# Pooled inputs made one block ahead on chip, first steps and units moved into the opening, scores by row quarters

## The chip, the cores and the metric

The kernel runs on one core of a Trainium2 chip. The metric is the device time of an execution in microseconds; lower is better. The engines are TensorE (PE, with its weight loads as PEld), VectorE (DVE), ScalarE (ACT), GpSimd (POOL) and SyncE (SP, which only issues DMAs here). Each works off its own queue of instructions in order and waits for others through semaphores.

## The reference, cut to what matters

The input x is 128 sequences of 32 tokens of 128 features. Four stages follow each other:

```
# 1 pooled: hidden = x; scores = tanh(x @ W1 + b1) @ v          per sequence
mask  = prefix / postfix / all-but-self, by the sequence's prompt type
pooled = softmax(where(mask, scores, -1e30)) @ x / cnt
# 2 attention of the pooled input, 16 heads of 8 and a rope part shared by the heads
c_kv = pooled @ W_kv_down;  k, v = c_kv @ W_k_up, c_kv @ W_v_up;  q = pooled @ W_q
scores = (q k + rope(pooled @ W_q_rope) rope(c_kv @ W_k_rope)) / sqrt(40), causal
x = x + (softmax(scores) @ v) @ W_o
# 3 per sequence one of 64 matrices:  c2 = x @ W[cat] + b[cat]
# 4 mixture of 64 experts on c2, and a shared one
s = sigmoid(c2 @ gate_w.T);  sc = s + gate_bias;  groups of 8: best 4 of 8 groups by top-2 sum
cw = top 8 of what is left, s normalised, times 2.5
x = x + sum_e cw[:, e] * ((silu(c2 @ Wg_e) * (c2 @ Wu_e)) @ Wd_e) + shared(c2)
```

## The kernel before

The tokens go in 8 blocks of 512 (16 sequences, 4 tiles of 128 tokens), features on the partitions. For each block the mixture is 33 **units** (`UNITS`): 32 pairs of experts and the shared expert. A unit p has a gate product, a down product (of unit p - 3, `NH = 3`) and an up product, each three full matmuls of 512 columns, since every float32 operand is split into a high and a low part (`three`). Gate goes to PSUM bank G0 or G1, up to U0 or U1, down is summed in Y. ScalarE takes silu of the gate in its bank (L520); VectorE multiplies by the routing weight (`act_w`, L938), which comes as `cwb`, a row of `cw_scratch` in DRAM spread over the partitions by a DMA, four slots (`NCW`) deep, then by the up product (`hid`, L950); ScalarE rounds `hid` to its high part (L532), GpSimd subtracts for the low part (`hid_lo`, L631).

The attention, conditioning and routing of block b + 1 run beside the units of block b, as 33 **steps** written out by hand. In unit p each engine does step p + 5 (`AHEAD = 5`) of the next block, behind its own work for the unit; units 28 to 32 do steps 0 to 4 of the block after it. `steps_in` gives this order to every engine, SP included. The steps: 0 rotation of the rope parts; 1 to 4 keys masked by head (`k_blk`, VectorE) and queries masked by group (`q_grp`, ScalarE); 5 value product and rope scores; 6 and 8 the scores of two tiles each (TensorE), 6 to 9 their mask, maximum and subtraction; 10 the exponentials; 12 to 16 turned probabilities and products with values, 13 to 16 `att`; 17 transposes; 18 output product and x2; 19 the product with the category's matrix (`wcat`, loaded in steps 13 to 16); 20 transposes and c2; 21 gate scores; 22 to 29 routing on VectorE; 31, 32 the weights `cw` turned and stored to DRAM.

The same steps for block 0 run alone in the **opening**, ahead of the units, with the pooling of all eight blocks between them: `pool_hidden`, `pool_scores`, `pool_weights` in three groups (block 0; 1 to 3; 4 to 7), then for each block `spread` (four 32x32 transposes on VectorE), `pool_out` (four products on TensorE) and `pooled_out` (a copy on ScalarE). For blocks 1 to 7 `pooled_out` stores to `pooled_scratch` in DRAM, and SP loads `h_feat` from it at step 21. Expert weights come in 24 parts of 256 KB and a small one; `split(i)` rounds part i on ScalarE and subtracts on GpSimd, 17 before the units (`BEFORE_UNITS`), the others one per unit from unit 11. `warm(n)` are products that nobody reads.

SP's queue is in order too: in unit p it does the loads of step p + 5 first, then waits for `weighted` and issues `cwb` of unit p:

```
for step, blk in steps_in(p, following, last):
    attention_loads(step, blk)
if p < NPAIR:
    sp.wait_ge(S["weighted"], b * NPAIR + (NPAIR + p - NCW + 1))
...
    sp.dma_start(cwb[:, p % NCW, :], src).then_inc(cwb_in[p % NCW], 16)
```

## Time and profile before

| | |
|---|---|
| median of 3 runs | 749.6 us (747.75 to 752.17) |
| the profiled execution, its own time | 748.22 us |
| span of its trace | 746.4 us |
| mean granted TensorE clock over the span | 0.995 |
| busy share PE / DVE / ACT / POOL | 97 / 74 / 61 / 57% |

Times in the trace are microseconds from the start of the span, durations of one instruction are nanoseconds where it says so. The granted clock is a share of full speed: 1.00 is 2.4 GHz, 0.50 is 1.2 GHz. A float32 matmul of this program appears as two MATMUL instructions; matmuls overlap, so the distance between starts is what one costs, and ends are modelled. The profiled execution is the source of all rows; its time lies 1.4 us under the median.

### The profile page before, as it was taken

The page shows a single profiled execution, that of the slowest core. Times are in us where ns is not written, and L with a number is a line of the kernel's source. Part 1 is how long each engine was busy: PE and PEld are TensorE (multiplying, and loading weights), DVE is VectorE, ACT ScalarE, POOL GpSimd, SP SyncE. Part 2 cuts the span into 40 slices and gives each one's busy share as a digit, 9 for nine tenths or more (in the row PEclk, how much of TensorE's full clock was granted, in tenths as well). Part 3 has the DMA queues.
Part 4 walks back from the last instruction along what each step waited for, and adds up shares of the span by engine and source line. Part 5 has one row for each costly group of instructions (what it writes and reads, how often), then busy time and mean ns, then how long its engine had stood idle before and what let it go on. Part 6 is the DMA issues. An engine that isn't in the chain of part 4 may idle for free.

```text
span 746.4 us, 15904 instructions
## 1 busy us (share of the span) xinstructions
PE 721.3 (97%) x5680; PEld 560.0 (75%) x5680; DVE 549.0 (74%) x1150; ACT 453.5 (61%) x873; POOL 425.1 (57%) x349
## 2 busy tenths in 40 slices
PE   8877999999999999999999999999999999999997
PEld 6765776677777777777787777777777777887885
DVE  5796668886698756976778766987668766886664
ACT  3755865477556675567555774566754675555553
POOL 2528667566456545655555654666446564566665
PEclk9999999999999999999999999999999999999999
DMA  7495443435534453444564344443634345345441
GB/s 264 141 356 135 123 121 99 127 94 156 120 107 118 123 144 109 129 103 127 125 117 134 98 150 113 120 113 120 141 113 135 103 125 128 102 125 141 128 134 46
DMA packets 69055, 97.21 MB, mean 130 GB/s; under 512 B 8016, under 2 KB 26896, under 8 KB 68976
## 3 DMA queue, kind: packets, MB, share of 16 engines
q1 hardware_dynamic: 64512, 91.21, 44.1%
q10 hardware_dynamic: 4464, 4.98, 1.9%
q8 instruction: 45, 0.74, 0.4%
q14 instruction: 34, 0.28, 0.1%
HBM read 90.73 MB, written 4.98 MB: 128 GB/s over the span
## 4 chain that ended last, share of the span: by engine, by line
PE 73%; DVE 11%; ACT 10%; issue 3%; POOL 2%; POOLq 0%; DVEq 0%; ACTq 0%
PE U L967 20%; PE Y L967 20%; PE G L967 19%; PE A L967 12%; DVE act_w L938 3%; POOL hid_lo L631 2%; ACT s_t L395 2%; ACT hid_hi L532 2%; DVE hid L950 2%; ACT L520 1%; ACT L395 1%; DVE k_blk L678 1%; ACT G L520 1%; PE A L1031 1%; DVE spread_p L861 1%
## 5 line engine op out<-in xcount | busy, mean ns | idle before, releaser
L631 POOL TENSOR_TENSOR hid_lo<-hid,hid_hi 128x512 fp32r<-128x512 f32 (+1 forms) x264 | 342.1, 1296 | 275.1 <-ACT hid_hi L532 274.0
L938 DVE TENSOR_TENSOR act_w<-G,cwb 128x512 f32<-128x512 f32 x248 | 170.4, 687 | 100.3 <-ACT G L520 99.3
L520 ACT ACTIVATE G<-G 128x512 f32<-128x512 f32 x248 | 144.4, 582 | 140.6 <-PE G L967 137.7
L532 ACT CAST hid_hi<-hid 128x512 fp32r<-128x512 f32 (+1 forms) x264 | 162.4, 615 | 71.8 <-DVE hid L950 70.5
L950 DVE TENSOR_TENSOR hid<-act_w,U 128x512 f32<-128x512 f32 (+1 forms) x256 | 175.8, 687 | 24.1 <-PE Y L967 1.5
L967 PE MATMUL Y<-hid_hi,wd_hi 128*128 128x512 f32 (+1 forms) x264 | 107.0, 405 | 5.4 <-POOL hid_lo L631 5.1
L967 PE MATMUL G<-c_hi,wg_hi 128*128 128x512 f32 x248 | 111.8, 451 | 0.2 <-DVE act_w L938 0.2
L967 PE MATMUL Y<-hid_hi,wd_lo 128*128 128x512 f32 (+1 forms) x264 | 103.6, 393 | 0.0
L967 PE MATMUL Y<-hid_lo,wd_hi 128*128 128x512 f32 (+1 forms) x264 | 103.4, 392 | 0.0
L967 PE MATMUL U<-c_hi,wu_hi 128*128 128x512 f32 x248 | 99.0, 399 | 1.1 <-DVE hid L950 1.1
L967 PE MATMUL G<-c_lo,wg_hi 128*128 128x512 f32 x248 | 97.5, 393 | 0.0
L967 PE MATMUL G<-c_hi,wg_lo 128*128 128x512 f32 x248 | 97.4, 393 | 0.0
L967 PE MATMUL U<-c_hi,wu_lo 128*128 128x512 f32 x248 | 97.4, 393 | 0.0
L967 PE MATMUL U<-c_lo,wu_hi 128*128 128x512 f32 x248 | 97.3, 392 | 0.0
L967 PEld LDWEIGHTS Y<-hid_hi,wd_hi 128*128 128x128 f32 (+1 forms) x264 | 49.5, 187 | 28.9 <-POOL hid_lo L631 16.7
L967 PEld LDWEIGHTS U<-c_hi,wu_hi 128*128 128x128 f32 x248 | 46.5, 188 | 17.0 <-DVE hid L950 4.4
L967 PEld LDWEIGHTS G<-c_hi,wg_hi 128*128 128x128 f32 x248 | 46.6, 188 | 16.4 <-issue 6.8
L967 PEld LDWEIGHTS Y<-hid_lo,wd_hi 128*128 128x128 f32 (+1 forms) x264 | 49.5, 188 | 11.2
L967 PEld LDWEIGHTS Y<-hid_hi,wd_lo 128*128 128x128 f32 (+1 forms) x264 | 49.6, 188 | 9.6
L967 PEld LDWEIGHTS G<-c_lo,wg_hi 128*128 128x128 f32 x248 | 46.5, 188 | 10.7
L967 PEld LDWEIGHTS U<-c_lo,wu_hi 128*128 128x128 f32 x248 | 46.5, 188 | 10.7
L967 PEld LDWEIGHTS U<-c_hi,wu_lo 128*128 128x128 f32 x248 | 46.5, 188 | 9.7
(191 smaller groups left out, 900.0 us busy)
## 6 DMA issues: line engine op xcount, KB each, us to landing
cwb<-cw_scratch SPq DMA_DIRECT2D x256, 256.0 KB, 3.7
k_blk<-in_cond_w SPq DMA_DIRECT2D x112, 64.0 KB, 2.4
wg_raw<-in_we_gate SPq DMA_DIRECT2D x8, 256.0 KB, 6.0
wu_raw<-in_we_up SPq DMA_DIRECT2D x8, 256.0 KB, 6.2
wd_raw<-in_we_down SPq DMA_DIRECT2D x8, 256.0 KB, 6.6
xf<-in_x_feat SPq DMA_DIRECT2D x8, 256.0 KB, 4.2
out_feat<-y ACTq DMA_DIRECT2D x8, 256.0 KB, 3.6
h_feat<-pooled_scratch SPq DMA_DIRECT2D x7, 256.0 KB, 2.7
```

Of the source, the lines that this page charges most:

```text
L395: nc.scalar.activation(s_t[:, t, :], s_t[:, t, :], ACT.Exp, scale=ATT_SCALE)\
L520: nc.scalar.activation(gate_bank(p)[:, :], gate_bank(p)[:, :], ACT.Silu).then_inc(S["silu_done"], 1)
L532: nc.scalar.copy(hid_hi[0:n, p % NH, :], hid[0:n, p % NH, :]).then_inc(S["hi_ready"], 1)
L631: nc.gpsimd.tensor_sub(hid_lo[0:n, p % NH, :], hid[0:n, p % NH, :], hid_hi[0:n, p % NH, :].bitcast(F32)).then_inc(S["lo_ready"], 1)
L678: nc.vector.tensor_scalar(k_blk[:, h, :], A1[:, :], C["head_of_group"][:, h:h + 1], None, ALU.mult)\
L861: last = nc.vector.transpose(pool_pt[i % 2][rows, :, s, :], pool_p[rows, bass.ts(i, TILES), :])
L938: nc.vector.tensor_mul(act_w[:, p % NH, :], gate_bank(p)[:, :], cwb[:, p % NCW, :])\
L950: nc.vector.tensor_mul(hid[0:n, p % NH, :], act_w[0:n, p % NH, :], up).then_inc(S["hid_ready"], 1)
L967: return nc.tensor.matmul(dst, lhsT, rhs, **k)
L1031: last = nc.tensor.transpose((G[1] if opening(blk) else A1)[:, bass.ts(g, P)], s_t[:, t, bass.ts(g, P)], C["ident"])
```

## The change

- Blocks 2 to 7 are pooled beside the units: block b's pooled input by `spread` in step 21, `pool_out` in step 24 and `pooled_out` in step 25 of block b - 1, straight to `h_feat`. The token rows for it are loaded by SP in step 21 into the buffer of `att`, once the transposes of step 20 have read it. `pooled_scratch` is gone.
- Block 1's pooled input is made after step 18 of block 0, and its first products, rotation, keys and queries run in steps 19 to 21 of block 0. In block 0 two of the four key masks go to ScalarE (from a second key product in G1), in block 1 all four.
- Units 0 and 1 of block 0 have their gate and up products before `cw` of block 0 is there. Their weights are spread by products with `pick` into Y and A1 (`first_weights`), not by DRAM. Step 6 of block 1 moves from unit 1 to unit 2.
- Scores: instead of four masked copies of q, one copy; each product takes 32 rows (one group of four heads) and has a tile position in rows and columns. Step 6 does groups 0 and 1 of all tiles, step 8 groups 2 and 3; in block 0 all at once into four banks. Step 8 waits for both tiles of step 6.
- 11 splits instead of 17 come before the units, the rest one per unit from 11 to 24; six weight loads are issued by ScalarE's queue. The fillers of steps 21 and 31 are gone. The loads of the categories come before those of x of blocks 1 to 7.

```diff
-        s_t = sb("s_t", [P, TILES, HEADS * SEQ])
+        s_t = sb("s_t", [P, NG, TILES * HG * SEQ])
...
-        q_grp = sb("q_grp", [P, NG, TOK])
+        q_sb = sb("q_sb", [P, TOK])
...
-        xt_in = [x_early[:, 4, :], x_early[:, 5, :], act_w[:, 2, :], hid[:, 2, :], y[:, :]] \
-            + [x_early[:, i, :] for i in range(3)]
-        pooled = [h_feat[:, :]] + [k_blk[:, i, :] for i in range(4)] + [act_w[:, 2, :], y[:, :], hid[:, 2, :]]
+        xt_in = [x_early[:, 4, :], x_early[:, 5, :]] + [att[:, :, :, :].rearrange("p t h d -> p (t h d)")] * (NBLK - 2)
...
-        pool_pt = [spread_p[:, i, :].rearrange("p (t s j) -> p t s j", t=TILES, s=SPT) for i in range(2)]
+        pool_pt = sb("pool_pt", [P, TILES, SPT, SEQ])
+        pool_p = sb("pool_p", [P, NBLK * TILES, SEQ])
...
-        h_dram = nc.dram_tensor("pooled_scratch", [P, NBLK * TOK], F32).ap()
...
-        BEFORE_UNITS = 17
-        SPLIT_UNITS = range(11, 11 + NSPLIT + 1 - BEFORE_UNITS)
+        BEFORE_UNITS = 11
...
-        WARM = {9: 4, 12: 2, 13: 2, 14: 2, 15: 2, 21: 24}
+        WARM = {9: 4, 12: 2, 13: 2, 14: 2, 15: 2}
...
+            sp.dma_start(cat_row[:, :], cats.to_broadcast([CATS, NSEQ])).then_inc(S["cats_in"], 16)
+            sp.dma_start(cat_table, cond_b).then_inc(S["cats_in"], 16)
+            sp.dma_start(gbias[:, :], gate_bias.to_broadcast([P, E])).then_inc(S["cats_in"], 16)
...
-                elif p == 21 and not (isinstance(blk, int) and blk == NBLK - 1):
...
-                    sp.wait_ge(S["wo_ps"], blk + 1)
-                    if opening(blk):
-                        sp.wait_ge(S["h_stored1"], 16)
-                    elif isinstance(blk, int) and blk == 1:
-                        for i in range(2, NBLK):
-                            sp.wait_ge(S[f"h_stored{i}"], 16)
+                elif p == 21 and 0 < blk < NBLK - 1:
+
+                    sp.wait_ge(S["c2_ps"], blk + 1)
                     sp.sem_inc(S["load_turn"], 1)
-                    sp.dma_start(h_feat[:, :], h_dram[:, bass.ds(blk * TOK + TOK, TOK)]).then_inc(S["h_in"], 16)
+                    token_load(blk + 1, "xt_in")
...
-            for i in range(1, 4):
-                token_load(i, "xt_in1")
+            token_load(1, "xt_in1")
...
+            for i in range(9, NSPLIT):
                 weight_load(i)
...
-                if p < NPAIR:
+                if p < NPAIR and (prev or p >= 2):
...
-                    if p == 0:
+                    if p == (0 if prev else 2):
...
+            def key_masks(heads, blk):
+
+                act.wait_ge(S["k_again_ps" if opening(blk) else "k_ps"], 1 if opening(blk) else blk + 1)
+                wait(act, "score_tile_ps", blk * TILES)
+                for h in heads:
+                    nc.scalar.mul(k_blk[:, h, :], (G[1] if opening(blk) else A1)[:, :], C["head_of_group"][:, h:h + 1]).then_inc(S["k_ready"], 1)
+
+            def pooled_out(i):
+
+                act.wait_ge(S["pooled_ps"], i + 1)
+                if i == 1:
+                    act.wait_ge(S["v_ps"], 1)
+                elif i >= 2:
+                    act.wait_ge(S["wo_ps"], i)
+                nc.scalar.copy(h_feat[:, :], (A0 if i == 0 else G[1] if i == 1 else A1)[:, :]).then_inc(S["pooled_ready"], 1)
...
-                    nc.scalar.mul(q_grp[:, p - 1, :], A2[:, :], C["group"][:, p - 1:p]).then_inc(S["q_ready"], 1)
+                        nc.scalar.copy(q_sb[:, :], A2[:, :]).then_inc(S["q_ready"], 1)
+                        if blk < 2:
+                            key_masks((range(2, HG), range(HG))[blk], blk)
...
+                elif p == 25 and 0 < blk < NBLK - 1:
+                    pooled_out(blk + 1)
...
-                act.dma_start(h_dram[:, bass.ts(i, TOK)], pooled[i]).then_inc(S[f"h_stored{i}"], 16)
...
+            for i in range(3, 9):
+                weight_load(i)
+            pooled_out(0)
...
                     pool_exp(1)
+                elif p == EXPS:
                     split(2)
                     split(3)
...
+                elif p == 19:
+                    split(6)
+                    pool_exp(2)
                 elif p == 20:
-                    pooled_out(2)
-                elif p == ROUND:
                     round_input(0, 0)
...
+                elif p == 21:
+                    split(7)
+            attention_step(1, 1)
+            for i in range(8, BEFORE_UNITS):
+                split(i)
...
+                    dst = act_w[:, p, :] if b == 0 and p < 2 else gate_bank(p)[:, :]
+                    nc.scalar.activation(dst, gate_bank(p)[:, :], ACT.Silu).then_inc(S["silu_done"], 1)
...
+                if p == 1 and not prev:
+                    attention_step(CWT, 0)
+                    attention_step(CWT + 1, 0)
...
+                if not prev and BEFORE_UNITS <= p <= NSPLIT:
+                    split(p)
...
+            for u in range(2):
+                for i in range(2):
+                    pair = C["ident"][:, E * i + 2 * u:E * i + 2 * u + 2].unsqueeze(1).to_broadcast([P, F, 2])
+                    last = nc.gpsimd.tensor_copy(pick[:, u, i, :].rearrange("p (f two) -> p f two", two=2), pair)
+            last.then_inc(S["pick_ready"], 1)
...
-                if 12 <= p < 17:
+                if 12 <= p < 18:
                     split(p - 10)
+            rope_add(1)
             pool.wait_ge(S["cw_ready"], 1)
-            for i in range(7, 10):
-                split(i)
...
+            for i in range(8, BEFORE_UNITS):
                 split(i)
...
+                    if h < 2 or blk >= 2:
+                        nc.vector.tensor_scalar(k_blk[:, h, :], A1[:, :], C["head_of_group"][:, h:h + 1], None, ALU.mult)\
+                            .then_inc(S["k_ready"], 1)
...
+                    dve.wait_ge(S["score_tile_ps"], TILES if opening(blk) else blk * TILES + t + 1)
...
+                        ps = first_scores[:, :, bass.ts(t, P)].rearrange("p g (h k) -> p g h k", k=SEQ)
+                        bias = rope_mask[:, t, :].unsqueeze(1).unsqueeze(1).to_broadcast([P, NG, HG, SEQ])
+                    else:
...
+                        ps = (A2, A1)[t % 2][:, :].rearrange("p (t h k) -> p t h k", h=HG, k=SEQ)
+                        bias = rope_mask[:, :, :].unsqueeze(2).to_broadcast([P, TILES, HG, SEQ])
+                    chain(nc.vector.tensor_add(s, ps, bias), blk)
+                    nc.vector.tensor_reduce(head_max[:, t, :], s_t[:, t, :].rearrange("p (n k) -> p n k", k=SEQ), AX, ALU.max)\
+                        .then_inc(S["biased_tile"], 1)
...
+                    if t == 0 and blk >= 2:
+                        dve.wait_ge(S["pooled_ps"], blk + 1)
...
+                elif p == 21 and 0 < blk < NBLK - 1:
+                    spread(blk + 1)
...
-                if p == 13:
-                    pool_scores(2)
+                if p == 9:
+                    pool_weights(1)
                 elif p == 16:
-                    pool_weights(1)
                     spread(1)
                 elif p == 18:
-                    spread(2)
-                    pool_weights(2)
+                    pool_scores(2)
...
+                    rotate(1)
+                    rest_of_input(0, 0)
+            pool_weights(2)
+            attention_step(0, 1)
...
-                    dve.wait_ge(cwb_in[p % NCW], b * (16 * NPAIR // NCW) + 16 * (p // NCW + 1))
-                    nc.vector.tensor_mul(act_w[:, p % NH, :], gate_bank(p)[:, :], cwb[:, p % NCW, :])\
+                    if b == 0 and p < 2:
+                        dve.wait_ge(S["cwb_ps"], p + 1)
+                        gate, weight = act_w[:, p, :], (Y, A1)[p]
+                    else:
+                        loaded = b * NPAIR // NCW + p // NCW + 1 - (1 if p % NCW < 2 else 0)
+                        dve.wait_ge(cwb_in[p % NCW], 16 * loaded)
+                        gate, weight = gate_bank(p)[:, :], cwb[:, p % NCW, :]
+                    nc.vector.tensor_mul(act_w[:, p % NH, :], gate, weight)\
...
+                pe.wait_ge(S["pooled_ready"], blk + 1)
...
+                if opening(blk):
+                    mm(G[1][:, :], k_w[:, :], h_feat[:, :]).then_inc(S["k_again_ps"], 1)
...
-                elif p in (6, 8):
...
-                            pe.wait_ge(S["biased_tile"], blk * TILES + t - 1)
...
-                                last = mm((A2, A1)[t % 2][32 * r:32 * r + 32, bass.ts(g, P)], q_grp[:, g, tok], k_blk[:, :, tok])
+                elif p == 6 and opening(blk):
+                    pe.wait_ge(S["rope_mask_ready"], 1)
+                    pe.wait_ge(S["k_ready"], HG)
+                    pe.wait_ge(S["tanh_done"], 2)
+                    for t in range(TILES):
+                        for r in range(SPT):
+                            tok = bass.ts(t * SPT + r, SEQ)
+                            for g in range(NG):
+                                rows = slice(32 * g, 32 * g + 32)
+                                last = mm(first_scores[32 * r:32 * r + 32, g, bass.ts(t, P)], q_sb[rows, tok],
...
+                elif p in (6, 8) and not opening(blk):
+                    pair = (p - 6, p - 5)
+                    if p == 6:
+                        pe.wait_ge(S["rope_mask_ready"], blk + 1)
+                        pe.wait_ge(S["k_ready"], blk * HG + HG)
+                        if blk == 1:
+                            pe.wait_ge(S["weighted"], NPAIR + 2)
+                    else:
+                        pe.wait_ge(S["biased_tile"], blk * NG + 2)
+                    for s in range(SPB):
+                        t, r = divmod(s, SPT)
+                        for g in pair:
+                            rows = slice(32 * g, 32 * g + 32)
+                            last = mm((A2, A1)[g % 2][32 * r:32 * r + 32, bass.ts(t, P)], q_sb[rows, bass.ts(s, SEQ)],
+                                      k_blk[rows, :, bass.ts(s, SEQ)], tile_position=(32 * g, 32 * r))
+                    last.then_inc(S["score_tile_ps"], 2)
...
-                    pe.wait_ge(S["prob_tile"], blk * TILES + t + 1)
+                    pe.wait_ge(S["prob_tile"], t + 1 if opening(blk) else blk * NG + NG)
...
+                elif p == 24 and 0 < blk < NBLK - 1:
+                    pool_out(blk + 1)
...
+                    pe.wait_ge(S["xt_in1"], 16)
+                    pe.wait_ge(S["biased_tile"], TILES)
+                else:
+                    pe.wait_ge(S["xt_in"], 16 * (i - 1))
+                    pe.wait_ge(S["c2tok_ready"], i)
+                dst = A0 if i == 0 else G[1] if i == 1 else A1
...
+            for p in range(CWT):
                 attention_step(p, 0)
-                if p == 7:
+                if p == 6:
...
+                elif p == 19:
+                    pe.wait_ge(S["pooled_ready"], 2)
+                    mm(G[0][:, :], rope_w[:, :], h_feat[:, :]).then_inc(S["rope_ps"], 1)
                 elif p == 21:
-                    pool_out(3)
-                    pool_out(4)
+                    mm(A1[:, :], k_w[:, :], h_feat[:, :]).then_inc(S["k_ps"], 1)
+                    pe.wait_ge(S["tanh_gate"], 1)
+                    mm(A2[:, :], W["q"], h_feat[:, :]).then_inc(S["q_ps"], 1)
...
+            def first_weights():
+
+                attention_step(CWT, 0)
+                pe.wait_ge(S["cwT_ready"], 1)
+                pe.wait_ge(S["k_ready"], 2 * HG)
+                pe.wait_ge(S["pick_ready"], 1)
+                for u in range(2):
+                    dst = (Y, A1)[u].rearrange("p (u two n) -> p two u n", two=2, n=P)
+                    for i in range(2):
+                        last = mm(dst[:, i], pick[:, u, i, :], cw_feat[:, :])
+                    last.then_inc(S["cwb_ps"], 1)
...
+                    if not prev:
+                        pe.wait_ge(S["rot_ready"], 2)
...
+                steps = steps_in(p, following, last)
+                if not prev and p == 1:
+                    first_weights()
+                    steps = []
+                elif not prev and p == 2:
+                    steps = steps_in(1, 1) + steps
+                for step, blk in steps:
```

## Rows read from the trace of the kernel before

**Rows 1.** The page, busy time by engine (share of the span)
```profile
PE 721.3 (97%) x5680; PEld 560.0 (75%) x5680; DVE 549.0 (74%) x1150; ACT 453.5 (61%) x873; POOL 425.1 (57%) x349
```

**Rows 2.** Busy time by stretch: start:end, length, busy (instructions), clock, DMA share, GB/s
```profile
0.00:64.34 64.34, 52.21 (x736) 43.01 (x737) 47.33 (x141) 35.40 (x78) 26.50 (x30) 0.97 0.69 229
79.66:162.85 83.19, 81.05 (x587) 60.69 (x583) 62.85 (x128) 53.16 (x101) 54.99 (x46) 1.00 0.42 117
342.57:429.33 86.76, 85.59 (x669) 66.00 (x665) 65.16 (x137) 53.93 (x103) 48.76 (x40) 1.00 0.49 122
429.33:509.29 79.96, 79.42 (x586) 61.34 (x582) 59.90 (x128) 49.62 (x91) 44.58 (x36) 1.00 0.45 123
```

**Rows 3.** Timeline of VectorE in the opening: start, us, line, operation
```profile
33.27 0.68 DVE L839 SCALAR_TENSOR_TENSOR hid<-act_w,G 128x512 f32<-128x512 f32 x1
...
41.38 0.69 DVE L708 TENSOR_TENSOR x_next<-A,xf 128x512 f32<-128x512 f32 x1
...
55.79 0.42 DVE L800 TENSOR_TENSOR cw<-rt,small 128x256 f32<-128x256 f32 x1
```

**Rows 4.** Timeline of TensorE in the opening
```profile
38.73 1.12 PE L967 MATMUL A<-h_feat,w 128*128 128x512 f32 x2 [0.68 <-ACT h_feat L403]
```

**Rows 5.** Timeline of ScalarE's queue, first store of the routing weights
```profile
58.31 1.32 ACTq L424 DMA_DIRECT2D cw_scratch<-cw_feat  x2
```

**Rows 6.** Timeline of SP's queue, block 0 and block 4
```profile
61.20 1.25 SPq L352 DMA_DIRECT2D cwb<-cw_scratch  x2
...
457.09 0.34 SPq L314 DMA_DIRECT2D h_feat<-pooled_scratch  x1
457.54 10.92 SPq L352 DMA_DIRECT2D cwb<-cw_scratch  x6
```

**Rows 7.** The line that loads `cwb` (L352), whole run
```profile
DMA to landing us min/median/max: 3.0/3.7/7.7
```

**Rows 8.** Busy time by stretch, opening (columns as in rows 2)
```profile
20.00:22.00 2.00, 0.45 (x32) 0.37 (x32) 1.97 (x4) 1.91 (x8) 1.59 (x2) 1.00 0.03 8
...
24.00:26.00 2.00, 2.00 (x44) 1.85 (x40) 1.08 (x2) 1.94 (x5) 0.00 (x0) 0.50 0.87 282
```

**Rows 9.** Timeline of TensorE in block 4
```profile
417.15 1.05 PE L967 MATMUL A<-v_w,h_feat 128*128 128x128 f32 x8
...
420.80 1.96 PE L967 MATMUL A<-k_blk,q_grp 128*32 128x128 f32 x64
...
427.44 1.95 PE L967 MATMUL A<-k_blk,q_grp 128*32 128x128 f32 x64
...
450.86 0.47 PE L967 MATMUL A<-v_blk,pt_sb 128*32 128x36 f32 x32
...
462.22 0.60 PE L1074 MATMUL A<-c,att 128*128 128x128 f32 x4
...
481.03 0.47 PE L967 MATMUL Y<-hid_hi,wd_hi 128*128 128x512 f32 x1
```

**Rows 10.** Timeline of VectorE in block 4
```profile
427.28 0.69 DVE L694 TENSOR_REDUCE head_max<-s_t 128x16 f32<-128x512 f32 x1
...
464.18 0.69 DVE L938 TENSOR_TENSOR act_w<-G,cwb 128x512 f32<-128x512 f32 x1 [0.46 <-ACT G L520]
...
467.16 0.69 DVE L938 TENSOR_TENSOR act_w<-G,cwb 128x512 f32<-128x512 f32 x1 [1.50 <-ACT G L520]
...
468.56 0.61 DVE L757 TENSOR_TENSOR rt<-biased 128x128 f32<-128x128 f32 x1
...
485.44 0.42 DVE L800 TENSOR_TENSOR cw<-rt,small 128x256 f32<-128x256 f32 x1
```

**Rows 11.** Timeline of VectorE in block 0
```profile
122.50 1.32 DVE L740 TENSOR_TENSOR rt<-rt 128x64 f32<-128x64 f32 x1
123.74 0.21 DVE L741 TENSOR_TENSOR rt<-rt 128x64 f32<-128x64 f32 x1
```

**Rows 12.** Timeline of GpSimd in block 0
```profile
122.45 1.29 POOL L597 TENSOR_TENSOR wd_lo<-wd_raw,wd_hi 128x512 fp32r<-128x512 f32 x1
```

More of the change, by code:

```diff
@@ L402, in attention_step @@
                     act.wait_ge(S["attT_ps"], blk + 1)
-                    nc.scalar.copy(att_feat[:, :], A1[:, :]).then_inc(S["attT_ready"], 1)
+                    nc.scalar.copy((y if opening(blk) else att_feat)[:, :], A1[:, :]).then_inc(S["attT_ready"], 1)
                 elif p == 19:
@@ L418, in attention_step @@
                     wait(act, "cw_stored", blk * 32)
-                    nc.scalar.copy(cw_feat[:, :], A0[:, 0:TOK // 2]).then_inc(S["cwT_ready"], 1)
+                    nc.scalar.copy(cw_feat[:, :], (Y if opening(blk) else A0)[:, 0:TOK // 2]).then_inc(S["cwT_ready"], 1)
                 elif p == CWT + 1:
@@ L481, in _ @@
             pool_hidden(1)
-            act.wait_ge(S["pooled_ps"], 1)
-            nc.scalar.copy(h_feat[:, :], A0[:, :]).then_inc(S["pooled_ready"], 1)
+            for i in range(3, 9):
+                weight_load(i)
+            pooled_out(0)
             split(0)
             split(1)
-            for p in range(UNITS):
+            for p in range(CWT):
                 attention_step(p, 0)
@@ L561, in unit @@
                     nc.scalar.copy(y[:, :], x2_next[:, :]).then_inc(S["x2_moved"], 1)
-            for p in range(AHEAD):
-                attention_step(p, 1)
-            pooled_out(5)
-            pooled_out(6)
             pipeline(unit)
@@ L618, in _ @@
                 attention_step(p, 0)
-                if 12 <= p < 17:
+                if 12 <= p < 18:
                     split(p - 10)
+            rope_add(1)
             pool.wait_ge(S["cw_ready"], 1)
-            for i in range(7, 10):
-                split(i)
-            rope_add(1)
-            for i in range(10, BEFORE_UNITS):
+            for i in range(8, BEFORE_UNITS):
                 split(i)
@@ L1030, in attention_step @@
                     for g in range(NG):
-                        last = nc.tensor.transpose((G[1] if opening(blk) else A1)[:, bass.ts(g, P)], s_t[:, t, bass.ts(g, P)], C["ident"])
+                        probs = s_t[:, t, bass.ts(g, P)] if opening(blk) else s_t[:, g, bass.ts(t, P)]
+                        last = nc.tensor.transpose((U[0] if opening(blk) else A1)[:, bass.ts(g, P)], probs, C["ident"])
                     last.then_inc(S["probT_ps"], 1)
@@ L1153, in _ @@
             pool_hidden(2)
-            for p in range(STEPS):
-                if p == CWT:
-                    warm(8)
+            for p in range(CWT):
                 attention_step(p, 0)
-                if p == 7:
+                if p == 6:
                     pool_scores(2)
@@ L1225, in unit @@
                         .then_inc(S["up_done"], 1)
-                if p == 0 and not prev:
-                    pool_out(7)
-                for step, blk in steps_in(p, following, last):
+                steps = steps_in(p, following, last)
[5 more added lines that the diff above has]
+                for step, blk in steps:
                     attention_step(step, blk)
```

191 lines of the change are left out of this document (59 added, 132 removed).

## The prediction, made before the change was run

> **What bounds the kernel now.** I read the page first: TensorE is busy 721.3 us, 97% of the span of 746.4 [rows 1]. Then the busy times by stretch [rows 2]. The cuts are the gate product of unit 4 in block 0 (79.66), that of unit 2 in block 1 (162.85), and the same two points in blocks 4 and 5 (429.33, 509.29). In that last stretch, of a block in its steady state, TensorE is busy 79.42 of 79.96 us: such a block costs the sum of its TensorE work. One whole block, unit 4 to unit 4, is 429.33 - 342.57 = 86.8 us. The opening is another matter: of the first 64.34 us TensorE is busy 52.21, fillers (`warm`) among it, and VectorE 47.33. And block 0 takes 83.19 where the steady block takes 79.96: 3.2 us more, with GpSimd busy 54.99 instead of 44.58. So the change can win or lose in three places: the opening, each block's TensorE sum, and stalls inside the blocks.
>
> **The opening.** In block 0 VectorE has pooling work between the steps of attention: `pool_scores(2)` from 33.27, three operations of 0.7, stands ahead of the adds of steps 14 to 16, and `pool_weights(1)` with `spread(1)` ahead of the add of step 18, which starts at 41.38 [rows 3] although its product ended at 38.73 + 1.12 = 39.85 [rows 4]. In the change both have left these places: 2.1 us from the first, 1.5 from the second, 3.6 for x2. `pool_weights(2)` (as many operations again) also leaves the way to c2; I take 4.1 for c2. The scores of block 0 in one lot are worth little: four VectorE adds and maxima per tile, 0.7 each, set the pace. SP's three category loads now go ahead of x of blocks 1 to 3, for which I have taken 1 us off. Routing then meets `rope_add(1)` on GpSimd, which holds one short operation up for 1.1 us (see block 0 below). The weights `cw`, now done at 55.79 + 0.42 = 56.2 [rows 3], come 3.2 us sooner, at 53.0.
>
> From `cw` to unit 4 the kernel takes 79.66 - 56.2 = 23.5 us. In the change units 0 and 1 have had their gate and up products before, the rotation, keys and queries of block 1 are done, and the weights of these two units come by four products instead of DMAs. What remains, counted from `cw`: VectorE is held by `pool_weights(2)` and a lock until +2.8, while transpose, copy and two `pick` products (an estimate: 1.7) run beside it; multiplies of two units and the rope mask, four of 0.69 less overlap, +5.3; scores +6.3; one score tile, 2 x 0.7, +7.7. Meanwhile unit 2's weights go by DRAM as now: `cw_scratch` issued at +0.9, the load 2.9 us after it (58.31 to 61.20 [rows 5, 6]), 0.5 for the issue, 3.7 to land [rows 7]: +8.0. It is then the last to come. Two multiplies, one tile, second scores: +11.8. The fillers are gone: after 2 us in which TensorE was busy 0.45, the granted clock fell to 0.50 (1.2 GHz of 2.4) [rows 8], and here TensorE has little from about 51 to 57: +0.5. Unit 4 starts at 53.0 + 12.3 = 65.3, **14.4 us earlier**.
>
> **Scores in every block.** Steps 6 and 8 are 64 matmul instructions each on four column tiles, 1.88 us from their start to the next matmul's, 29 ns apiece (the rows' 1.96 has a modelled end) [rows 9]. In the change the same 64 use 32 rows each: eight tiles. The trace has nothing on different row tiles at once. Bounds: no gain (1.88), and the pace of the smallest matmuls seen, 32 in 0.47 us, 15 ns apiece, 0.94 [rows 9]. I take 1.0, since each tile streams half as much and the issue pace allows it. By the Trainium skill, TensorEngine Tiling, Key Properties and Gotcha 1, tiles work in parallel as long as row tiles write different PSUM banks, and the pair goes to A2 and A1. By that rule it is 0.94, by the row of the scores alone 1.88; no row here shows it.
> Not all is kept. Step 8 starts at 427.44 today [rows 9] and needs only the first tile by then; in the change it waits for both, and VectorE ends the second at 427.28 + 0.69 = 427.97 [rows 10]. What is ahead of it moves up with TensorE's 0.9 us from step 6, to 427.1; TensorE, ready at 426.55, waits 0.55. Net **-1.1 us** for each of attention blocks 2 to 7, which run beside unit blocks 1 to 6.
>
> **Pooling, moved from the opening into blocks 0 to 5.** `pool_out` is four products; the nearest row is 8 instructions in 1.05 us [rows 9]. `spread`, four transposes of 0.3, fits into VectorE's idle 1.50 us before 467.16 [rows 10] if nothing else is late. `pooled_out` is one copy on ScalarE, which gives back three of four query copies; neither bounds.
> What is late is a load. At unit 16 SP waits before it issues that unit's `cwb`. Today it waits for the product of step 18: h_feat is issued at 457.09, `cwb` at 457.54 [rows 6]; it lands 3.7 us on, at 461.2, and the multiply of unit 16 is at 464.18 [rows 10]: 2.9 us to spare. In the change SP waits there for `c2_ps`, the transposes of step 20, 462.22 + 0.60 = 462.8 [rows 9]: 5.8 us later. The token load goes first, `cwb` at 463.4, landed at 467.1. The multiply slips by 2.9 us. Behind it on VectorE stand hid of unit 16, `spread` (its free slot is gone), both multiplies of unit 17 and routing, 4.1 us after it: at 471.2 instead of 468.56. From 468.56 to the last `cw` (485.44) VectorE shows no idle time [rows 10], so it can't catch up, and TensorE's margin is down to nothing at 481.03, where it takes the down product as hid_lo ends [rows 9]. TensorE loses **2.6 us** in each of blocks 0 to 5; the 1.05 us of `pool_out` fall inside that time and are not added.
>
> **Block 0.** Only 11 splits come before the units instead of 17; the rest run in units 11 to 24, not 11 to 18. A routing operation that takes 0.21 elsewhere takes 1.32 [rows 11] while GpSimd subtracts (122.45, 1.29 us [rows 12]). The six more splits fall under units 19 to 24, where I count three such short operations, 0.6 each: +1.8. By the Trainium skill, SBUF, the section on the shared port, the port pair is locked for a whole instruction; by that each of them could wait 1.29, +3.9. Block 0: 1.8 + 2.6 = **+4.4**.
>
> **Sum.** -14.4 + 4.4 + 5 x (2.6 - 1.1) - 1.1 = -3.6 us on 746.4. The profiled execution took 748.2, 1.8 over its span; the median of the runs shown is 749.6. I put the sum on the median: **746.0 us**.
>
> **Rivals.**
> - *The load is hidden after all.* Blocks 1 to 5 then change by 1.05 - 1.1, block 0 by +1.8, block 6 by -1.1: -14.0 in all, **735.6**. For it: 2.9 us to spare today. Against: the release is 5.8 us later. It needs a landing within 0.8 us of the issue; the shortest seen is 3.0 [rows 7].
> - *Slower: row tiles don't overlap.* Steps 6 and 8 stay at 1.88 and step 8 waits 0.55: +0.55 instead of -1.1 in six blocks (+9.9); the opening's 128 instructions take 3.8 instead of 1.7 (+2.1): **758**. It decides if 64 instructions take over 1.6 us. For it: no row of such overlap. Against: on four column tiles instructions of 128 columns do follow each other at 29 ns.
> - *GpSimd bounds block 0.* A split and a hid_lo are 2.6 us per unit against 2.1 of TensorE's, in eight units, and GpSimd waits for VectorE besides: another +5, **751**. For it: the 3.2 us that block 0 loses already.
>
> **Chances.** The forecast 0.47 (own range 742 to 750), the hidden load 0.22, the tiles 0.11, GpSimd 0.20. The range is 735 to 757. Under 0.5% (3.75 us) a change can't be told from none here. Faster than 745.85: all of the second case and 0.23 of the first, 0.45; within: 0.24 of the first and 0.14 of GpSimd's, 0.38; slower 0.17.
>
> **What would show it.** Right: the gate product of unit 4 near 65; 64 score instructions in about 1 us; at unit 16 SP released by the transposes and VectorE idle for 2 to 3 us before act_w, ended by a DMA; blocks 1 to 5 at 88.3 us instead of 86.8, unit 4 to unit 4; short routing operations of 1.3 us as late as unit 24 of block 0. Wrong: steady blocks under 86, no wait for `cwb`, scores still at 1.88, or a clock under 1.00 beyond the first units.

## The result, and the profile after

The changed kernel takes **754.5 us** (median of 17 runs, 751.2 to 757.5) against 748.1 for the kernel before on the same chip (17 runs): ratio 1.0076, 95% interval 1.0061 to 1.0092. It is 0.8% slower. I had forecast 746.0, slightly faster; 754.5 lies inside the range of 735 to 757, but on the other side of no change. The profiled execution has a span of 750.8 us (746.4 before). Its own time, 752.6, lies 1.8 us under its median, so the two traces show 4.4 us of the 6.4 between the medians; where the other 2.0 lie no trace here tells.

Cut at the same points as before (gate product of unit 4 in block 0, of unit 2 in block 1, of unit 0 in block 7), busy time by stretch, first the kernel before where [rows 2] has no such stretch:

```profile
162.85:671.77 508.92, 504.58 (x3861) 389.66 (x3858) 382.27 (x798) 317.26 (x602) 287.30 (x230) 1.00 0.45 122
671.77:746.40 74.63, 70.02 (x304) 56.30 (x302) 46.81 (x68) 38.28 (x70) 45.17 (x35) 0.98 0.41 112
```

and the changed kernel:

```profile
0.00:70.86 70.86, 52.64 (x837) 39.70 (x837) 47.67 (x128) 38.65 (x90) 31.57 (x37) 0.95 0.57 176
70.86:159.10 88.24, 82.79 (x595) 60.34 (x591) 65.98 (x131) 55.06 (x104) 61.55 (x51) 1.00 0.48 116
159.10:676.36 517.26, 504.99 (x3902) 383.68 (x3897) 386.60 (x818) 309.95 (x593) 287.47 (x231) 1.00 0.46 119
676.36:750.80 74.44, 69.98 (x304) 56.28 (x302) 46.81 (x68) 38.33 (x70) 45.14 (x35) 0.98 0.38 115
```

| stretch | before | after | change | forecast |
|---|---|---|---|---|
| start to unit 4 of block 0 | 79.66 | 70.86 | -8.8 | -14.4 |
| to unit 2 of block 1 | 83.19 | 88.24 | +5.05 | +4.4 |
| to unit 0 of block 7 | 508.92 | 517.26 | +8.3 | +6.4 |
| to the end | 74.63 | 74.44 | -0.2 | 0 |
| sum | 746.4 | 750.8 | **+4.4** | **-3.6** |

Of the 8.0 us between the two sums 5.6 lie in the opening. In the third stretch TensorE is busy for as long as before (505.0 and 504.6 us) while the stretch is 8.3 us longer: 7.9 of them are waiting.

**The late `cwb`.** Block 4, timeline of SP's queue, then of VectorE, against [rows 6, 10]:

```profile
464.18 0.34 SPq L270 DMA_DIRECT2D att<-in_x_tok  x1
464.63 9.79 SPq L332 DMA_DIRECT2D cwb<-cw_scratch  x7
```

```profile
468.65 0.69 DVE L936 TENSOR_TENSOR act_w<-banks,cwb 128x512 f32<-128x512 f32 x1 [3.66 <-DMA cwb<-cw_scratch]
469.45 0.69 DVE L948 TENSOR_TENSOR hid<-act_w,banks 128x512 f32<-128x512 f32 x1
470.05 1.24 DVE L866 STREAM_TRANSPOSE pool_pt<-pool_p 32x128 f32<-32x128 f32 x4
471.33 0.69 DVE L936 TENSOR_TENSOR act_w<-banks,cwb 128x512 f32<-128x512 f32 x1
472.12 0.69 DVE L948 TENSOR_TENSOR hid<-act_w,banks 128x512 f32<-128x512 f32 x1
472.73 0.28 DVE L762 TENSOR_TENSOR rt<-biased 128x128 f32<-128x128 f32 x1
```

SP issues the token load and then `cwb` of unit 16 at 464.63 instead of 457.54; VectorE stands idle for 3.66 us, ended by that DMA; `spread` and the routing queue behind it. The routing starts 4.2 us later than in [rows 10] by the clock of the trace; counted from the gate product of unit 4 (430.56 here, 429.33 before) it is 2.9 us, where I had 2.6. The list of SP's waits (in total, times, longest) has the place; before, the longest at that place was 5.5 us:

```profile
SPq L301 <- PE banks L1090: 67.8, 6, 11.4
```

**The scores**, TensorE, block 4, against the 1.88 us from start to the next matmul in [rows 9]: here 1.08 (429.48 to 430.56), after a wait of 0.52 for the second tile.

```profile
429.48 1.15 PE L965 MATMUL banks<-k_blk,q_sb 32*32 32x128 f32 x64 [0.52 <-DVE head_max L694]
430.56 0.50 PE L965 MATMUL banks<-c_hi,wg_hi 128*128 128x512 f32 x1
```

**The opening.** TensorE's products on x of blocks 1 to 3; then VectorE; then GpSimd; then TensorE around `cw`:

```profile
11.11 1.39 PE L965 MATMUL banks<-x_early,w 128*32 128x128 f32 x24 [2.91 <-DMA x_early<-in_x_feat]
```

```profile
41.48 0.69 DVE L711 TENSOR_TENSOR x_next<-banks,xf 128x512 f32<-128x512 f32 x1 [1.46 <-PE banks L965]
...
44.84 0.69 DVE L714 TENSOR_TENSOR c<-banks,cat_bias 128x512 f32<-128x512 f32 x1 [0.62 <-PE banks L1090]
...
50.15 1.34 DVE L762 TENSOR_TENSOR rt<-biased 128x128 f32<-128x128 f32 x1 [2.60 <-POOL biased L578]
...
58.18 0.43 DVE L805 TENSOR_TENSOR cw<-rt,small 128x256 f32<-128x256 f32 x1
```

```profile
48.15 1.28 POOL L586 TENSOR_TENSOR wu_lo<-wu_raw,wu_hi 128x512 fp32r<-128x512 f32 x1 [2.32 <-ACT wu_hi L438]
49.39 0.73 POOL L578 TENSOR_TENSOR biased<-score,gbias 128x256 f32<-128x256 f32 x1
50.08 1.26 POOL L567 TENSOR_TENSOR rope_sum<-pt_sb 64x512 f32<-64x512 f32 x1
```

```profile
58.75 0.41 PE L1104 MATMUL banks<-c,cw 128*128 128x128 f32 x2 [3.19 <-DVE cw L805]
59.62 3.39 PE L965 MATMUL banks<-cw_feat,pick 128*128 128x256 f32 x8 [0.46 <-ACT cw_feat L418]
```

`cw` is done at 58.6, 2.4 us later than in [rows 3] and 5.6 later than my 53.0. c2 is made from 44.84 on, and the routing starts only at 50.15: GpSimd subtracts weight tile 7 before it makes the biased scores, and then adds the rotated halves (`rope_add(1)`) while the first routing operation runs, which takes 1.34 us where the like operation behind it (L763) takes 0.28.

### The profile page after: what moved, and what is told of

The parts are those of the page before. It is cut to its first block, busy times and chain, and to the rows that moved or that the text cites. A ratio compares the mean times of both kernels' runs of the same rounds, so it can differ in the third digit from the quotient of the medians.

```text
span 750.8 us, 15764 instructions
## 1 busy us (share of the span) xinstructions
PE 710.4 (95%) x5626; PEld 540.0 (72%) x5626; DVE 547.1 (73%) x1144; ACT 442.0 (59%) x854; POOL 425.7 (57%) x352
## 4 chain that ended last, share of the span: by engine, by line
PE 63%; DVE 16%; ACT 8%; issue 4%; DMA 4%; POOL 3%; SPq 1%; POOLq 0%; DVEq 0%
PE banks L965 60%; DVE act_w L936 5%; DMA cwb<-cw_scratch 4%; DVE hid L948 3%; POOL hid_lo L623 2%; ACT s_t L392 2%; ACT hid_hi L526 2%; ACT L514 1%; ACT L392 1%; ACT banks L514 1%; PE banks L1047 1%; DVE head_max L694 1%; DVE s_t L693 1%; DVE pool_pt L866 1%; DVE rt L768 1%
## 5 line engine op out<-in xcount | busy, mean ns | idle before, releaser
L936 DVE TENSOR_TENSOR act_w<-banks,cwb 128x512 f32<-128x512 f32 x254 | 174.6, 687 | 138.7 <-ACT banks L514 112.7
L514 ACT ACTIVATE banks<-banks 128x512 f32<-128x512 f32 x254 | 147.2, 582 | 127.7 <-PE banks L965 125.7
L948 DVE TENSOR_TENSOR hid<-act_w,banks 128x512 f32<-128x512 f32 (+1 forms) x264 | 181.3, 687 | 23.7 <-PE banks L965 1.5
L965 PE MATMUL banks<-c_hi,wg_hi 128*128 128x512 f32 x264 | 120.8, 458 | 7.9 <-DVE act_w L936 7.9
L965 PE MATMUL banks<-hid_hi,wd_hi 128*128 128x512 f32 (+1 forms) x264 | 107.7, 408 | 5.4 <-POOL hid_lo L623 5.2
L965 PE MATMUL banks<-c_hi,wg_lo 128*128 128x512 f32 x264 | 103.7, 393 | 0.0
L965 PE MATMUL banks<-c_lo,wg_hi 128*128 128x512 f32 x264 | 103.7, 393 | 0.0
L965 PE MATMUL banks<-hid_hi,wd_lo 128*128 128x512 f32 (+1 forms) x264 | 103.7, 393 | 0.0
L965 PE MATMUL banks<-hid_lo,wd_hi 128*128 128x512 f32 (+1 forms) x264 | 103.5, 392 | 0.0
L965 PE MATMUL banks<-c_hi,wu_hi 128*128 128x512 f32 x256 | 102.2, 399 | 0.3 <-DVE hid L948 0.3
L965 PEld LDWEIGHTS banks<-hid_hi,wd_hi 128*128 128x128 f32 (+1 forms) x264 | 49.5, 187 | 30.9 <-POOL hid_lo L623 19.1
```

The costliest lines, as they stand in the source:

```text
L514: nc.scalar.activation(dst, gate_bank(p)[:, :], ACT.Silu).then_inc(S["silu_done"], 1)
L936: nc.vector.tensor_mul(act_w[:, p % NH, :], gate, weight)\
L948: nc.vector.tensor_mul(hid[0:n, p % NH, :], act_w[0:n, p % NH, :], up).then_inc(S["hid_ready"], 1)
L965: return nc.tensor.matmul(dst, lhsT, rhs, **k)
```

## The experiments

Ratios are to the kernel before, measured beside each experiment; "unit 4", "unit 8" are the starts of these gate products in block 0, "block 0" the time from unit 4 to unit 2 of block 1.

**1. `cwb` first.** At unit 16 of the changed kernel SP's order is turned round.

```diff
-    for step, blk in steps_in(p, following, last):
-        attention_loads(step, blk)
+    if p != 16:
+        for step, blk in steps_in(p, following, last):
+            attention_loads(step, blk)
     if p < NPAIR and (prev or p >= 2):
...
+    if p == 16:
+        for step, blk in steps_in(p, following, last):
+            attention_loads(step, blk)
```

> The changed kernel, but at unit 16 SP issues that unit's cwb load before it waits for c2_ps and loads the tokens. Theory (the late cwb costs 2.6 us in each of blocks 0 to 5, and hides 1.05 us of pool_out): the idle time of VectorE before act_w(16), 3.66 us in block 4, falls under 0.5 us, the blocks from the gate product of unit 0 to the next are 1.5 us shorter (88.3 to 86.8 in block 4), 9 us in all: 745 us, ratio to the kernel before 0.997. Rival (spread and the two products of pool_out bound these blocks whatever the load does): under 3 us shorter, 752 or more.

Measured: **740.2 us**, ratio 0.9894 [0.9866, 0.9921], 14 us under the changed kernel and 1.1% faster than the kernel before. Busy time by stretch:

```profile
73.19:157.10 83.91, 81.66 (x596) 61.00 (x591) 64.69 (x131) 55.07 (x104) 62.11 (x51) 1.00 0.52 120
157.10:664.29 507.19, 500.22 (x3901) 385.54 (x3897) 387.32 (x818) 311.79 (x592) 287.73 (x231) 1.00 0.48 122
```

VectorE's idle time before act_w(16) in block 4 is 0.46 us, ended by ScalarE. From block 1 to block 7 it gives back 10.1 us, 2.0 for each of the five blocks (I had 1.5), and in block 0 alone 4.3; 14 us in all by the medians, against the 9 expected (12 by the traces, of which this one has an opening 2.3 us longer). The rival is out. The wait for the transposes has moved to `cwb` of unit 17, which now stands behind the token load, and there it costs less:

```profile
460.60 0.69 DVE L940 TENSOR_TENSOR act_w<-banks,cwb 128x512 f32<-128x512 f32 x1 [0.48 <-DMA cwb<-cw_scratch]
```

**2. The same wait in the kernel before.** There SP loads h_feat at step 21; it now waits for the transposes of step 20 (in block 0 of the attention it stays).

```diff
-    sp.wait_ge(S["wo_ps"], blk + 1)
+    sp.wait_ge(S["wo_ps" if opening(blk) else "c2_ps"], blk + 1)
```

> The kernel before with one edit: in blocks 1 to 6 SP waits at step 21 for c2_ps, as the changed kernel does, and no longer for wo_ps, before it loads h_feat and then cwb of unit 16. Theory (the later wait alone makes cwb late and costs each of blocks 0 to 5 about what the experiment with cwb first gave back there, 2 us): VectorE idle for 2 to 3.7 us before act_w(16), the blocks 2 us longer, 12 us in all: 760, ratio 1.016. Rival (it costs only together with spread, which took VectorE's free slot): under 1 us in each block, 754 or less.

Measured: 757.7 us, ratio 1.0136 [1.0113, 1.0159]. VectorE waits for the same load:

```profile
474.45 0.69 DVE L938 TENSOR_TENSOR act_w<-G,cwb 128x512 f32<-128x512 f32 x1 [3.29 <-DMA cwb<-cw_scratch]
```

Blocks 1 to 6 take 7.5 us more, 1.5 for each of five; block 0 only 0.7 (83.86). Another 2.1 us were lost in this execution's opening, which the edit doesn't touch (below). So the wait alone does most of it, without `spread`: the theory, at 8 us in the trace and not 12 (the medians differ by 9.6). But it doesn't do the 4.3 us of block 0.

**3. Block 0: GpSimd relieved, without and with the late `cwb`.** ScalarE copies the weights in the place of GpSimd's difference for tiles 11 to 23; the true low parts of these weights are left out.

```diff
     nc.scalar.copy(hi, raw).then_inc(S["split_hi"], 1)
+    if i >= BEFORE_UNITS:
+        act.wait_ge(S["split_lo"], i)
+        nc.scalar.copy(lo, raw).then_inc(S["split_lo"], 1)
...
 def split(i):
+    if BEFORE_UNITS <= i < NSPLIT:
+        return
     pool.wait_ge(S["split_hi"], i + 1)
```

> The changed kernel with cwb of unit 16 first, and GpSimd relieved in block 0: for the weight tiles 11 to 23 a copy of the weights by ScalarE stands in the place of GpSimd's difference, so the low parts of these weights are not what they should be and the time of ScalarE grows by 0.6 us in each of 13 units. Theory (GpSimd's splits lengthen short VectorE operations of the routing from 0.2 to 1.3 us): block 0 from the gate product of unit 4 to that of unit 2 in block 1 falls from 83.9 to 81, total 737. Rival (they cost nothing that TensorE sees): 83.9 and 740.

> The changed kernel, late cwb and all, with GpSimd relieved in block 0: for the weight tiles 11 to 23 a copy by ScalarE stands in the place of GpSimd's difference, so the low parts of these weights are not what they should be. The late cwb costs block 0 4.3 us (88.2 against 83.9 from the gate product of unit 4 to that of unit 2 in block 1) where a steady block loses 2.0 and block 0 of the kernel before with the late wait lost 0.7. Theory (the splits in units 11 to 24 are what keeps VectorE and GpSimd from catching up): 84.5 to 85.5 here, 3 us or more off, total 751. Rival (late cwb and splits add up, 1.3 us for the splits as in the experiment without the late cwb): 87, total 753.

Measured with `cwb` first: 736.4 us, ratio 0.9851 [0.9826, 0.9875]; from unit 8 to unit 2 of block 1, where the opening's clock no longer plays in, 73.7 instead of 75.1 us: 1.3 off, not the 3 expected. With the late `cwb`: **748.2 us**, ratio 1.0010 [0.9990, 1.0030], 6 us under the changed kernel; block 0 as a stretch:

```profile
70.55:153.93 83.38, 81.62 (x596) 60.75 (x591) 61.22 (x131) 61.50 (x117) 45.46 (x38) 1.00 0.53 122
```

That is 4.9 us less than the 88.24 of the changed kernel, and more than the theory had. The four kernels, from unit 8 to unit 2 of block 1 in us:

| | GpSimd's splits | relieved |
|---|---|---|
| late `cwb` | 79.40 | 74.53 |
| `cwb` first | 75.06 | 73.74 |

The late load costs 0.8 without the splits (0.7 in the kernel before with the late wait) and 4.3 with them; the splits cost 1.3 without the late load and 4.9 with it; both together 5.7. They don't add up. The starts of the gate products show where: counted from unit 8, the changed kernel and the one with `cwb` first are level at unit 17 (27.4 us), 1.9 us apart at unit 20 (36.7 and 34.8), 3.3 at unit 24 (48.2 and 44.9) and 4.4 at unit 27 (57.8 and 53.4), while the two relieved kernels are 0.8 apart at unit 19 and stay so. It isn't how busy GpSimd is (61.6 us in the stretch, and 62.1 in the shorter one with `cwb` first), nor the long routing operations by themselves: between units 17 and 28 eight of them take over 0.6 us in the changed kernel, 7.9 us together, and seven, 6.3 us together, with `cwb` first; yet TensorE's waits there are 4.9 us in the first and 1.3 in the second. My reading, which no run separates further: the long operations cost TensorE something only once the late load has used up VectorE's lead.

**4. The category loads behind x of blocks 1 to 3**, where they were before (three `dma_start` lines moved to `i == 4`).

> The changed kernel with the three category loads behind x of blocks 1 to 3, as in the kernel before. Theory (they are why x lands 1.9 us later, which I priced at 1 us): TensorE's wait for x_early ends near 9.3 us instead of 11.1, h_feat is copied 1.5 to 2 us earlier, the weights cw are done near 57 instead of 58.6, and the whole is 1.5 us shorter: 753. Rival (the category loads hold up something else when they come later, or GpSimd's order before the routing takes the gain): no change at cw, 754.5.

Measured: 751.9 us, ratio 1.0034 [1.0016, 1.0053]: 2.6 us less by the medians, as the theory had it; by its profile `cw` is 1.9 us earlier and unit 4 1.1, but unit 8 no earlier at all (79.70), and the span is 750.9. These two profiles don't show what the runs do: this one lies 0.8 us over its median, that of the changed kernel 1.8 under. How far it is the loads can be read over all profiled executions: the 24 products on x of blocks 1 to 3 start at 11.1 to 12.2 us in the eight with the category loads ahead (h_feat copied at 16.1 to 18.2), and at 9.2 to 10.9 in the six with them behind (14.3 to 17.3). About 1.7 us, under a scatter of nearly the same size: in experiment 2, whose opening is that of the kernel before, h_feat came at 17.33 instead of 14.27.

**5. GpSimd's order.** rope_add(1) ahead of the biased add, split 7 behind `cw`.

```diff
+    if p == 20:
+        rope_add(1)
     attention_step(p, 0)
-    if 12 <= p < 18:
+    if 12 <= p < 17:
         split(p - 10)
-rope_add(1)
 pool.wait_ge(S["cw_ready"], 1)
-for i in range(8, BEFORE_UNITS):
+for i in range(7, BEFORE_UNITS):
     split(i)
```

> The changed kernel, but on GpSimd in the opening rope_add(1) goes ahead of the biased add, and split 7 goes behind cw, with splits 8 to 10. Theory (routing of block 0 is late by GpSimd's order): the first routing operation starts near 48.9 instead of 50.15 and takes 0.3 instead of 1.34, cw is done near 56.3 instead of 58.6, the gate product of unit 4 comes 2.3 us earlier, 68.6 instead of 70.9, total 752. Rival (the four splits behind cw, 5 us of GpSimd, hold hid_lo of unit 0 and the multiplies up): unit 4 not earlier than 70, total 754 to 755.

Measured: 753.6 us, ratio 1.0073 [1.0049, 1.0097], no change by the runs. The routing does start at 48.48 and its first operation takes 0.29 us; `cw` is done at 55.88, 2.7 us earlier, and unit 4 at 69.78, but unit 8 at 79.82. Of the 2.7 us 0.9 are c2, which this execution has at 43.91; the edit's own part is 1.8 (from c2 to `cw` 12.0 us instead of 13.8). Busy time by stretch shows where it went; the clock is the third column from the end:

```profile
54.00:56.00 2.00, 0.00 (x0) 0.01 (x1) 1.83 (x7) 1.46 (x5) 0.04 (x1) 0.83 0.00 0
56.00:58.00 2.00, 1.52 (x4) 1.05 (x5) 1.90 (x4) 0.37 (x1) 2.00 (x2) 0.50 0.00 0
...
66.00:68.00 2.00, 0.31 (x2) 0.00 (x0) 1.86 (x4) 0.97 (x3) 1.01 (x2) 1.00 0.24 62
68.00:70.00 2.00, 1.67 (x65) 1.29 (x66) 1.68 (x4) 0.72 (x3) 1.96 (x2) 0.74 0.37 122
70.00:72.00 2.00, 2.00 (x5) 1.59 (x6) 1.26 (x2) 0.54 (x1) 0.00 (x0) 0.50 0.38 117
```

Twice TensorE has nothing to do for 2 us or more, and twice the granted clock falls to 0.50 (1.2 GHz of 2.4). The second time it waits for the score tiles ahead of step 8, and the products of unit 4 then take 0.63 us instead of 0.40.

**6. Fillers.** Products of 128 columns nobody reads, ahead of the rope scores of block 1, ahead of the transposes of `cw`, and (in the second of the three) ahead of step 8.

> The changed kernel with cwb of unit 16 first, and fillers on TensorE: 22 of 128 columns ahead of the rope scores of block 1 and 26 ahead of the transposes of cw, 0.11 us each. Theory (in the experiments without them the clock fell to 0.50 for 6 to 11 us, at a different place each time, and took away what an edit of the opening had gained): the clock stays at 1.00 from 44 to 66, the eight pick products take 1.7 instead of 3.4 us, the gate product of unit 4 comes at 69 to 70.5 instead of 73.2, total 738. Rival (cw and the load of cwb(2) set unit 4 at any clock): unit 4 at cw + 12.3 as before, total 740.

> The changed kernel as it is, late cwb and all, with fillers in the three places: 10 ahead of the rope scores of block 1, 12 ahead of the transposes of cw, 6 ahead of step 8 of block 1. Theory (leaving the fillers out cost the opening two spells at half the clock): the clock at 1.00 from 44 to 80, the pick products 2.0 instead of 3.4 us, the gate product of unit 8 at 78 instead of 79.7, total 752 to 753. Rival (the opening is bound by VectorE and the load of cwb(2), and the fillers only take TensorE's time): 79.7 or later, 754.5 or more.

> The kernel before with the 24 fillers of step 21 left out, one part of the change alone. Theory (they hold the clock through the routing of block 0): the clock falls to 0.50 somewhere between 55 and 70 for 4 to 10 us, and the gate product of unit 4 comes 1.5 to 3 us later than 79.7, total 750 to 751. Rival (the forecast's half microsecond, since VectorE and the loads set this stretch): 80.2 or less, 748.6.

The first missed: 744.8 us, ratio 0.9962 [0.9945, 0.9979], 4 us worse than without fillers. A filler takes 0.22 us, not the 0.11 that I had read off a grouped row whose count is not one per product: the transposes came 4.5 us late for them, and the clock still fell at 73, ahead of step 8. With the right numbers, on the changed kernel: the clock stays at 1.00 from 44 to 82 and the pick products take 1.99 us instead of 3.39; yet 753.6 us, ratio 1.0062 [1.0043, 1.0081], within the uncertainty of the changed kernel's 1.0076. And the kernel before without its 24 fillers is as fast as with them: 748.3 us, ratio 1.0004 [0.9990, 1.0019], with a clock of 0.50 from 58 to 64 and unit 4 at 79.67. Leaving the fillers out cost nothing that these runs can tell, there or here.

**7. One row quarter after the other.** In steps 6 and 8 the loops over row quarters and sequences are exchanged; the instructions are the same 64.

```diff
-for s in range(SPB):
-    t, r = divmod(s, SPT)
-    for g in pair:
+for g in pair:
+    for s in range(SPB):
+        t, r = divmod(s, SPT)
```

> The changed kernel, but in steps 6 and 8 of blocks 1 to 7 the 32 matmuls of the first row quarter are all issued before the 32 of the second, instead of in turn; work and results are the same. Theory (the gain from 1.88 to 1.08 us for 64 instructions comes from two row quarters at work at once, which needs them in turn): 64 instructions take 1.8 to 1.9 us again, 0.8 us more in each of 14 steps, 11 us in all: 765. Rival (an instruction on 32 rows is shorter by itself, or the order does not matter): still 1.1 us for 64, 754.5.

Measured: 759.4 us, ratio 1.0148 [1.0122, 1.0173], 5 us more than the changed kernel, between the two. In block 4:

```profile
434.05 1.56 PE L965 MATMUL banks<-k_blk,q_sb 32*32 32x128 f32 x64 [0.49 <-DVE head_max L694]
435.54 0.50 PE L965 MATMUL banks<-c_hi,wg_hi 128*128 128x512 f32 x1
```

64 instructions in 1.49 us, 23 ns apiece: of the 0.80 us gained over 1.88, half needs the turns and half does not. With the quarters the PSUM bank (A2 or A1) takes turns too; whether the second half comes from two quarters at work at once or from the change of bank, this run doesn't separate.

**8. All together.** `cwb` first, category loads behind, GpSimd's new order, and pool_weights(2) on VectorE ahead of the routing instead of behind `cw`, where it held the multiplies up; fillers too many, then fewer.

```diff
                     rest_of_input(0, 0)
+                    pool_weights(2)
-            pool_weights(2)
```

> The changed kernel with everything that paid or should: cwb of unit 16 first, the category loads behind x of blocks 1 to 3, rope_add(1) ahead of the biased add with split 7 behind cw, pool_weights(2) ahead of the routing, and fillers (4 and 24). Theory (each takes its own part off the opening once the clock is held): cw done near 55.5, the gate product of unit 4 at 66 to 68, total 735. Rival (the opening is bound elsewhere, by the load of cwb(2) or by GpSimd behind cw): unit 4 not before 69.5, total 738 or more.

> All the edits that paid together, with fillers of the length that the last runs showed (0.22 us each, not 0.11): 3 ahead of the rope scores of block 1, 14 ahead of the transposes of cw, and 6 more ahead of step 8 of block 1, into the up bank of unit 2 once hid of unit 2 is done. Theory (the 24 fillers held the transposes up by 1.4 us, and the idle time before step 8 cost the clock from 67 to 74): cw done at 55, the gate product of unit 4 at 67 to 67.5, of unit 8 at 76 to 77 instead of 80.2, total 734 to 735, ratio 0.982. Rival (six fillers after 1.6 us of idle time don't hold the clock): it falls to 0.50 at 68 again, unit 8 at 78.5 or later, total 736.5 to 738.

Measured: 738.0 us, ratio 0.9873 [0.9851, 0.9895], and **736.2 us, ratio 0.9835 [0.9814, 0.9856]**, the fastest version that leaves nothing out: 1.6% under the kernel before, 2.4% under the changed one. The first has `cw` at 54.91 but loses the clock at 67 and reaches unit 8 at 80.15; the second has `cw` only at 56.83 (its h_feat came 0.65 us later, and its clock was at 0.50 from 32 to 34), keeps the clock after that, and has unit 8 at 78.08, 1 us later than its theory.

## Why the prediction was wrong, point by point

- **The opening, "-14.4 us", is the step that failed** (-8.8): the weights `cw` that I put at 53.0. All of the miss is `cw` at 58.6 instead of 53.0. From `cw` to unit 4 I had 12.3 us, and it took 12.25 (partly by luck: `pick` took 3.4 us at half clock and not 1.7, under pool_weights(2), and no wait for `cwb(2)`, which I had as the last to come, shows in the trace). Up to c2 I had 4.1 us gained and 0.4 came (44.84 against 45.20 before). The pooling did leave VectorE's way, but h_feat was 3.2 us late: 1.9 from x, where I had allowed 1 us for the loads, the rest from `pool_hidden(1)` and the steps behind it at half clock. And from h_feat to c2 the moved pooling gave 3.5 us (27.4 instead of 30.9), where my 4.1 has 5.1 in it before the 1 us for the loads. Experiment 4 shows the direction of the loads' part; its size sinks in the scatter of the openings. From c2 to `cw` I had 0.9 us lost and it was 2.8 (13.8 instead of 11.0): I counted the lock by rope_add(1) (priced at 1.1, though only 0.9 went into the 3.2 for `cw`), and missed that split 7 stands ahead of the biased add. Experiment 5 took back 1.8 of the 2.8.
- **An earlier `cw` carries over to unit 8 only where the clock holds**, which no step of mine looked at. From `cw` to unit 8 it took 21.1 to 21.3 us in the changed kernel, in experiment 3 with the late `cwb` and in the two kernels with fillers in all three places; in all four the clock was at 1.00 in the wait ahead of step 8 and behind it. It took 23.0 and 23.9 in experiments 4 and 5, where it fell there, and 22.5 in experiment 1, which kept it there but had it at 0.50 from 54 to 64. These are single executions: that the clock is the cause is read off them, not tested.
- **The late load, "2.6 us in each of blocks 0 to 5", stood**, with its place and its mechanism: SP released by the transposes, VectorE idle for 3.66 us, ended by the DMA. VectorE waited longer than the 2 to 3 us that I named (3.7 to 4.8 in blocks 1 to 5), and the loss is smaller than 2.6: as the difference that `cwb` first makes, 2.0 in a steady block. As the sum has it (blocks 1 to 5 at +1.5 each) it came to 8.6 / 5 = 1.7. Read back, experiment 1 is my rival "the load is hidden after all": its steady block, 422.61 - 336.01 = 86.60 us, is what I gave it, 86.8 less 0.05 (the mean of its five is 86.2, against 86.6 in the kernel before). It came out at 740.2 and not 735.6, by the opening again.
- **Block 0, "1.8 + 2.6 = +4.4"**, was right as a sum (+5.05) by luck and wrong as a sum of parts. By experiment 3 the load alone costs 0.8 and the splits alone 1.3, and together 5.7. The rival "GpSimd bounds block 0", another 5 us on top of the 4.4, did not come.
- **The scores, 1.0 us for 64**, took 1.08, with the 0.5 us wait for the second tile; block 6, which has nothing else of the change, is 1.03 us shorter against my 1.1. By the Trainium skill, TensorEngine Tiling (Array Packing), Key Properties and Gotcha 1, different tiles can work in parallel, row tiles only on different PSUM banks; experiment 7 agrees with that for half of the gain. The rival "row tiles don't overlap" is out by its own mark, 1.6 us for 64, which even the version with one quarter after the other (1.49) stays under.
- **Fillers, "+0.5"**: by experiment 6 too small to be told from nothing (ratio 1.0004 [0.9990, 1.0019] for leaving 24 of them out).

What stays open: why the clock fell in the wait ahead of step 8 in experiments 4 and 5 and not in the changed kernel, whose wait was as long (2.0 us), nor in experiment 1, whose wait was 2.9; and what sets the time at which x of blocks 1 to 3 lands from one execution to the next. One execution of each was profiled. I had read the fall of the clock off the stretch from 20 to 22 us, with 0.45 us of TensorE work [rows 8]; the same trace has another with as little, after which the clock stays:

```profile
72.00:74.00 2.00, 0.45 (x9) 0.25 (x10) 1.78 (x3) 0.60 (x3) 0.85 (x1) 1.00 0.79 207
74.00:76.00 2.00, 2.00 (x10) 1.64 (x10) 0.21 (x1) 0.97 (x2) 0.00 (x0) 1.00 0.40 121
```

## What to carry to other kernels

Look at what stands behind a wait in the same queue: one line of order in SP, `cwb` before the token load, was worth 14 us, twice the loss that the change had brought. Put the wait for a shared buffer (here att, which also takes the next tokens) behind the loads that have a deadline and not ahead of them. And price costs that meet in one stretch together: block 0 had 0.8 and 1.3 us to lose on two counts alone, and lost 5.7 on both.

## What the runs showed of the hardware

- 64 float32 matmuls of 128 columns on four column tiles: 1.88 us (29 ns apiece) on 128 rows in the kernel before, 1.49 (23 ns) on 32 rows with one row quarter after the other, 1.08 (17 ns) on two quarters and two PSUM banks in turn.
- At one place of the program TensorE waited for 2.0 us in each of these executions: the clock was then at 0.50 for some 3.4 us in experiments 4 and 5 and stayed at 1.00 in the changed kernel. From `cw` to unit 8 the first two took 2 to 3 us longer.
- GpSimd's addition (1.26 us) lengthened a VectorE operation with two inputs that ran beside it from 0.28 to 1.34 us. By the Trainium skill, SBUF — State Buffer, "Who interferes with whom", the one that comes second waits for the whole instruction of the other; the row agrees.
